# Normalised rows and the first two decoding steps, computed by ScalarE in place of VectorE

## What is computed

```python
x = _layernorm(x + attn(x))          # 16 heads of 8 channels, causal, q and k rms-normed and rotated
x = _layernorm(x + ffn(x))
# ffn: xn = rmsnorm(x) * norm_w; q = xn @ w_q.T
#      per head: top 8 of 32 scores on each of two sides, top 8 of their 64 sums -> fs, expert number fi
#      hidden = gelu(xn . expert_down[fi]) * relu(fs);  out = sum of hidden * expert_up[fi]
# _layernorm(x) = (x - mean) / sqrt(var + 1e-5)
```

## Time and profile before

| | us |
|---|---|
| three runs | 1857.17, 1856.44, 1856.55 (median 1856.55) |
| the profiled execution | 1853.35 |
| its span, first to last instruction | 1851.6 |
| granted TensorE clock, mean | 0.819 |

### The profile page before, as it was taken

One profiled execution on the slowest core, in us unless ns is written; L12 is line 12 of the kernel. 1 busy time (PEld: TensorE's weight loads), 2 busy tenths in 40 slices (PEclk: granted clock), 3 DMA queues, 4 the chain that ended last, 5 costly groups with the idle time before them and its releaser, 6 DMA issues. The chain is left out here.

```text
span 1851.6 us, 53652 instructions
## 1 busy us (share of the span) xinstructions
PE 1331.8 (72%) x19632; PEld 922.5 (50%) x19632; DVE 1554.3 (84%) x7082; ACT 891.2 (48%) x1518; POOL 732.0 (40%) x1088
## 2 busy tenths in 40 slices
PE   3557687685877768597776959678685867868646
PEld 2333364563555455455544636455463645546436
DVE  2148999888998888889888898988889898898995
ACT  1656645445554544555454455545455554554110
POOL 1125363433445343344434344442444434353230
PEclk9778789796978969697896969879697987979665
DMA  2000000000000000000000000000000000000000
GB/s 74 1 7 8 7 10 7 15 7 15 8 1 16 7 15 7 15 8 1 16 7 15 8 7 10 7 16 7 15 8 2 15 7 16 1 14 2 8 1 14
DMA packets 30049, 19.61 MB, mean 11 GB/s; under 512 B 1824, under 2 KB 29216, under 8 KB 29728
## 3 DMA queue, kind: packets, MB, share of 16 engines
q1 hardware_dynamic: 29728, 15.23, 3.0%
HBM read 11.04 MB, written 4.19 MB: 8 GB/s over the span
## 5 line engine op out<-in xcount | busy, mean ns | idle before, releaser
L579 ACT ACTIVATE prob<-S 128x512 f32<-128x512 f32 x640 | 368.7, 599 | 436.2 <-PE S L749 270.1
L841 PE MATMUL G<-whot,onehot 128*128 128x16 bf16 x12288 | 379.3, 172 | 59.2 <-DVE hid L1233 24.3
L841 PEld LDWEIGHTS G<-whot,onehot 128*128 128x128 bf16 x12288 | 365.2, 100 | 91.9 <-issue 37.4
L1195 DVE TENSOR_TENSOR onehot<-lo_no,esel 128x1024 bf16<-128x1024 uint16 x512 | 387.2, 811 | 0.1
L747 PE MATMUL S<-qT,kT_even 128*128 128x512 bf16 (+3 forms) x512 | 153.0, 329 | 146.0 <-issue 100.3
L416 POOL TENSOR_TENSOR qk_a<-qk_n,cosw 128x256 f32<-128x256 f32 x64 | 58.1, 908 | 470.4 <-DVE qk_n L1012 433.9
L462 POOL TENSOR_TENSOR gat<-gat,cande 128x1280 f16<-128x1280 f16 x64 | 151.5, 2367 | 212.1 <-DVE gat L1156 212.1
L699 PE MATMUL S<-ident_b,stack 128*128 128x128 bf16 x1024 | 100.0, 270 | 146.6 <-POOL stack L432 113.4
L749 PE MATMUL S<-causal,ident_b 128*128 128x128 bf16 x1024 | 205.4, 233 | 0.0
L699 PEld LDWEIGHTS S<-ident_b,stack 128*128 128x128 bf16 x1024 | 84.1, 124 | 185.8 <-POOL stack L432 138.2
L1136 DVE FIND_INDEX8 topi<-topv,sims 128x8 uint16<-128x32 f32 x1024 | 166.2, 187 | 0.3 <-issue 0.3
(11 more groups left out here) (139 smaller groups left out, 2578.3 us busy)
## 6 DMA issues: line engine op xcount, KB each, us to landing
xa<-in_L_attn_x SPq DMA_DIRECT2D x16, 256.0 KB, 2.7
xr<-in_L_attn_x SPq DMA_DIRECT2D x16, 256.0 KB, 3.4
out<-r SPq DMA_DIRECT2D x16, 256.0 KB, 2.4
onehot<-in_L_ffn_expert_down SPq DMA_DIRECT2D x1, 512.0 KB, 6.0
up<-in_L_ffn_expert_up SPq DMA_DIRECT2D x1, 512.0 KB, 7.1
onehot<-in_L_ffn_keys SPq DMA_DIRECT2D x1, 256.0 KB, 6.4
onehot<-in_L_attn_w_qkv SPq DMA_DIRECT2D x1, 192.0 KB, 4.8
onehot<-in_L_attn_w_proj SPq DMA_DIRECT2D x1, 64.0 KB, 4.7
```

What stands on the lines that cost most here:

```text
L579: act.activation(dst, src, ACT.Exp, scale=SCALE).then_inc(exp_done.sem, 1)
L841: last = nc.tensor.matmul(bank[:, 16 * i:16 * i + 16], onehot[:, pair, t, :], whot[:, t, w_part, :], start=(w_part == 0), stop=(w_part == 2))
L1195: dve.tensor_tensor(onehot[:, pair, t:t + 8, :].rearrange("p t (c i) -> p t c i", i=2), lo, e, ALU.is_equal)
```

## The change

Three pieces of work go from VectorE to ScalarE:

1. The kept rows of the first norm and the output rows of the second: in place of (row - mean) * root on VectorE, ScalarE computes root * row + shift with `Identity`, its scale and its bias both columns of 128x1. The shift is -mean * root, one new VectorE instruction of 128x4 for each norm: in `norm1` behind the rows `yi`, and behind `normalise(nxt, 1)` for the second. ScalarE's eight instructions stand behind the first four exponentials of group 0, first `oldest`, then `late`.
2. The first two steps of `decode`: ScalarE's `selection(late)`, a copy to integers and a Relu, stands behind the 40th exponential of b and ahead of `attended(b, 3)`. VectorE's first step of `decode` is now the mask L1180, behind a wait for ScalarE.
3. ScalarE's loop begins at b = 3 in place of 2, since its iteration now names `oldest` too. The last batch's output rows are ScalarE's too.

```diff
+            def selection(b):
+                act.wait_ge(f_ready.sem, f_filled(b, "sel"))
+                act.wait_ge(hot_done.sem, hot_done.value(b, 0))
+                bank = bank_f("sel")
+                n = 2 * P
+                act.activation(eint.rearrange("p a t c -> p (a t) c"),
+                               bank[:, 0:n].unsqueeze(2).to_broadcast([P, n, 2]), ACT.Copy)
+                act.activation(wpart[:, 0].rearrange("p a t c -> p (a t) c"),
+                               bank[:, n:2 * n].unsqueeze(2).to_broadcast([P, n, 2]), ACT.Relu).then_inc(dec.sem, 1)
...
+            def norm1_rows(b):
+                act.wait_ge(shift1_done.sem, shift1_done.value(b, 1))
+                act.wait_ge(kept.sem, kept.value(b, 0))
+                for t in range(NT):
+                    last = act.activation(y_new[:, t, :], r1[:, t, :], ACT.Identity, scale=rs[:, 0, t:t + 1],
+                                          bias=shift1[:, t:t + 1])
+                last.then_inc(ln1.sem, 1)
+
+            def norm2_rows(b):
+                act.wait_ge(shift2_done.sem, shift2_done.value(b, 1))
+                for t in range(NT):
+                    last = act.activation(r2[:, t, :], r2[:, t, :], ACT.Identity, scale=qk_rs[:, 64 + t:65 + t],
+                                          bias=shift2[:, t:t + 1])
+                last.then_inc(out_ready.sem, 1)
...
                 for g in range(NG):
                     if b is not None:
                         exps(b, g, range(4))
+                    if g == 0 and oldest is not None:
+                        norm2_rows(oldest)
+                    if g == 0 and late is not None:
+                        norm1_rows(late)
+                    if b is not None:
                         if g:
                             attended(b, g - 1)
                         exps(b, g, range(4, SIMS_UNIT + 2))
...
                     if b is not None:
                         exps(b, g, range(SIMS_UNIT + 2, UNITS))
+                if late is not None:
+                    selection(late)
                 if b is not None:
                     attended(b, NG - 1)
...
-            def norm1_rows(b):
-
-                dve.wait_ge(kept.sem, kept.value(b, 0))
-                for t in range(NT):
-                    last = dve.tensor_scalar(y_new[:, t, :], r1[:, t, :], mv[0][:, t, 0:1], rs[:, 0, t:t + 1],
-                                             ALU.subtract, ALU.mult)
-                last.then_inc(ln1.sem, 1)
+                dve.scalar_tensor_tensor(shift1[:, :], mv[0][:, :, 0], -1.0, rs[:, 0, :], ALU.mult, ALU.mult)\
+                    .then_inc(shift1_done.sem, 1)
...
+            def norm2_shift(b):
+                dve.scalar_tensor_tensor(shift2[:, :], mv[1][:, :, 0], -1.0, qk_rs[:, 64:64 + NT], ALU.mult, ALU.mult)\
+                    .then_inc(shift2_done.sem, 1)
...
-                dve.wait_ge(f_ready.sem, f_filled(b, "sel"))
-                dve.tensor_copy(pairs(eint[:, :, :, :]), twice(e))
-                dve.tensor_scalar(w0, twice(w), 0.0, None, ALU.max).then_inc(dec.sem, 1)
                 dve.wait_ge(dec.sem, dec.value(b, 1))
...
-                if oldest is not None:
-                    norm2_rows(oldest)
-                if late is not None:
-                    norm1_rows(late)
...
                 if nxt is not None:
                     normalise(nxt, 1, older, beside=hot(18, 20))
+                    if older is not None:
+                        norm2_shift(older)
```

More of the change, by code:

```diff
@@ L119, in attention_then_peer_layer @@
         rs_t = sb("rs_t", [P, 2, NT], fp32)
+        shift1 = sb("shift1", [P, NT], fp32)
+        shift2 = sb("shift2", [P, NT], fp32)
         y_new = sb("y_new", [P, NT, D], fp32)
@@ L226, in attention_then_peer_layer @@
         yi_done = signal("yi_done", 1)
+        shift1_done = signal("shift1_done", 1)
+        shift2_done = signal("shift2_done", 1)
         f_ready = signal("f_ready", 14)
@@ L241, in attention_then_peer_layer @@
         hi_done = signal("hi_done", 4)
-        hot_done = signal("hot_done", 4)
+        hot_done = signal("hot_done", 4, 4)
         g_ready = signal("g_ready", 8)
@@ L249, in attention_then_peer_layer @@
         out_ready = signal("out_ready", 1)
-        seeded = [out_stored, sims_done, hid_done, kept, rot_done, stack_done, exp_done, pv_done, oT_done, ln1, dec, ln2, cand_done, top1_done, g_free]
+        seeded = [out_stored, sims_done, hid_done, kept, rot_done, stack_done, exp_done, pv_done, oT_done, ln1, dec, ln2, cand_done, top1_done, g_free, hot_done]
         peak_ready = signal("peak_ready", NT * NH)
@@ L586, in attended, with iteration @@
                 act.activation(oT, OV[:, :], ACT.Copy).then_inc(oT_done.sem, 1)
-            def iteration(b, late, older, nxt):
+            def norm1_rows(b):
[11 more added lines that the diff above has]
+                last.then_inc(out_ready.sem, 1)
+            def iteration(b, late, older, oldest, nxt):
                 for g in range(NG):
@@ L641, in iteration @@
                     transposed(nxt, 3)
[L643 to L650, removed]
+            iteration(None, None, None, None, 0)
+            iteration(0, None, None, None, 1)
+            iteration(1, 0, None, None, 2)
+            iteration(2, 1, 0, None, 3)
+            with act.Fori(3, BATCH - 1) as b:
+                iteration(b, b - 1, b - 2, b - 3, b + 1)
+            iteration(BATCH - 1, BATCH - 2, BATCH - 3, BATCH - 4, None)
+            iteration(None, BATCH - 1, BATCH - 2, BATCH - 3, None)
+            iteration(None, None, BATCH - 1, BATCH - 2, None)
+            norm2_rows(BATCH - 1)
         @block.tensor
@@ L1115, in norm2_root @@
                              b - (BATCH - 3), 0)
[L1117 to L1122, removed]
             def top_keys(b, t):
@@ L1172, in decode @@
                 flat = lambda a: a.rearrange("p a t c -> p (a t c)")
-                e, w = bank[:, 0:n], bank[:, n:2 * n]
+                w = bank[:, n:2 * n]
                 w0, w1, w2 = (pairs(wpart[:, i]) for i in range(3))
                 rest = wrest[:, :, :].rearrange("p a t -> p (a t)")
-                dve.wait_ge(f_ready.sem, f_filled(b, "sel"))
-                dve.tensor_copy(pairs(eint[:, :, :, :]), twice(e))
-                dve.tensor_scalar(w0, twice(w), 0.0, None, ALU.max).then_inc(dec.sem, 1)
                 dve.wait_ge(dec.sem, dec.value(b, 1))
@@ L1328, in _ @@
             iteration(None, None, BATCH - 1, BATCH - 2, None)
-            norm2_rows(BATCH - 1)
 _INS = ["L0_attn_x", "L0_attn_w_qkv", "L0_attn_w_proj", "L0_attn_q_norm_w", "L0_attn_k_norm_w", "L0_ffn_w_q",
```

## The result

The changed kernel takes 1900.02 us (median of four runs, 1893.27 to 1906.24), the kernel before 1856.49 (1856.04 to 1857.17): 43.5 us more, a ratio of 1.0233 with a 95% interval of 1.0198 to 1.0269. The forecast was 1904 in a range of 1891 to 1920. The profiled execution of the changed kernel is the slowest of the four, 1906.24 us with a span of 1904.4 and a granted TensorE clock of 0.802 (before: 0.819).

What follows compares the result with a forecast made beforehand. The prediction took a closed path through TensorE, ScalarE, VectorE and GpSimd as the bound, not VectorE's busy time. Terms 44.7 + 1.5 + 3 - 2.05 - 0.2, then +0.2, gave +47 us: 1904 us, range 1891 to 1920.

Steps and rivals of the forecast that it cites:

- The five pieces: One loop iteration's closed path: scores to decode 43.59 us, VectorE 35.22, GpSimd 13.62, TensorE's weights 8.62, its loop turn 8.13.
- The rows on VectorE: Loop start: removing eight row instructions (2.05 us) only lengthens the wait for G, gain 0; 2.05 gained once, last iteration but one.
- The rows on ScalarE: Eight instructions behind group 0's fourth exponential, 0.35 us each, mostly covered by idling before the fifth: +3 us, ends 0 and +10.
- a sign that it was wrong: Signs included the fifth exponential later by more than a microsecond, or TensorE's clock lower between last `attend` and the transposes.
- The shift: One more 128x4 VectorE instruction in `norm1`, on the path: 0.1 us fifteen times, +1.5 us.
- The two decode steps: On ScalarE behind the 40th exponential, they start VectorE's mask 2.98 us later in each of 15 iterations: +44.7 us.
- A: Rival: VectorE is the bound, so work removed from it makes the kernel faster, about 1813 us; chance 0.05.
- B: Rival: no change, the selection's 3.0 us are absorbed by slack, about 1857 us; chance 0.04.
- C: Rival: TensorE idles 3 us more before the projections and falls to 1.2 GHz more often: +22, 1926 us; chance 0.05.
- D: Rival: Relu and Identity need extra ScalarE table loads at the rows and the selection: +58, 1962 us; chance 0.02.
- E: Rival: some iterations have another path, so only half of the selection's 3.0 us counts: +23, 1880 us; chance 0.04.
- The wait's length: VectorE's wait on ScalarE ahead of the mask L1180 was to appear in 15 iterations at 5 to 6 us.

Runs made afterwards that it cites:

- sel_only: The kernel before with only the two decode steps moved to ScalarE, behind the 40th exponential, rows still on VectorE: 1898.36 us, ratio 1.0233.
- extra_path: `rows_only` plus three useless 128x512 reductions on VectorE behind one-hot 11, in the 15 iterations with attention: 1880.54 us, 26.9 above `rows_only`.
- reorder_rows: `rows_only` with four one-hots taken out of VectorE's piece between decode and L1012, the second pair's 16 behind quarters 0 and 1: 1819.73 us, ratio 0.9811.
- rows_only: The changed kernel with both decode steps back on VectorE, rows and shifts still on ScalarE: 1853.66 us, ratio 0.9984 to the kernel before.
- reorder_only: The kernel before, rows on VectorE, with the one-hot order of `reorder_rows`: 1824.68 us, ratio 0.9836 to the kernel before.
- the pair of extras: `rows_only` with three useless VectorE reductions, behind one-hot 11 (1880.54 us) or at the start of VectorE's iteration (1856.29 us).

## Why the prediction was right, point by point

**What bounds the kernel.** The five pieces and their lack of slack held. A delay or a saving of 2 to 3 us in the first piece (`sel_only`) or in the second (`extra_path`, `reorder_rows`) showed in the iteration's sum with its size, and the other pieces stayed within 0.4 us.

**The rows on VectorE, 0 in the loop.** Right: the iteration of `rows_only` is not shorter, and its wait for G is longer. The gain outside the loop was mis-sized: 2.05 in the sum, 6.3 us in the traces of before and `rows_only`. The step that failed is the count of places without cover. I counted the last iteration but one; in the iterations of b = 2 and b = 15 VectorE did not wait for G either in the kernel before, and there the mask comes 2.2 and 1.2 us sooner behind the first exponential in `rows_only` (43.6 for 45.8, 42.1 for 43.3). A part of the difference is not the rows' at all: before, L855 took 9.28 us in the iteration without a next batch and VectorE waited 1.17 for it, a wait that the trace of `rows_only` lacks.

**The rows on ScalarE, +3 us.** The size of one was right, and the wait that was to cover them was misread. ScalarE's timeline at the loop's start in the changed kernel:

```profile
810.00 0.60 ACT L595 ACTIVATE prob<-S 128x512 f32<-128x512 f32 x1 [0.58 <-PE S L789]
810.49 1.64 ACT L615 ACTIVATE r<-r,shift,qk_rs 128x128 f32<-128x128 f32 x4
812.03 1.64 ACT L608 ACTIVATE y_new<-xr,shift,rs 128x128 f32<-128x128 f32 x4
813.56 0.58 ACT L595 ACTIVATE prob<-S 128x512 f32<-128x512 f32 x1
814.34 0.60 ACT L595 ACTIVATE prob<-S 128x512 f32<-128x512 f32 x1 [0.20 <-PE S L789]
```

Eight instructions take 3.07 us, 0.384 each; the prediction had 0.35. The Trainium skill, page "ScalarE: Activation LUTs", section "What ACT_TABLE_LOAD costs", gives 186 ns plus 0.833 ns per element, 93 ns more for each column operand and an overlap of 93 ns; the estimate by that is 479 ns of duration and 386 between starts, and the trace agrees: 0.48 and 0.384.

The prediction took both rows for the fifth exponential. They are the sixth. In the iteration at 780 the fifth is at 786.19, and ScalarE idled 0.68 us ahead of it, not 2.47; TensorE then makes two similarity products before the sixth score (ScalarE's and TensorE's timelines of the kernel before):

```profile
786.19 0.60 ACT L579 ACTIVATE prob<-S 128x512 f32<-128x512 f32 x1 [0.68 <-PE S L749]
```

```profile
786.63 2.06 PE L795 MATMUL F<-simW,xn 128*128 128x512 f32 x2
```

So the rows do delay the fifth exponential. Counted from the first one it starts 5.72 us behind in the kernel before and 8.13 in the changed kernel and in `rows_only` (means of the loop's twelve iterations). That is 2.4 us later, where the prediction had named more than a microsecond as a sign that it was wrong. The delay is absorbed one step on, in the long wait ahead of the sixth (2.47 before, 0.20 in the lines above): the sixth is 0.5 us later (8.80 in `rows_only`, 8.31 before), the 40th 0.2 (45.59 and 45.42). The other pair with the same order of work, `reorder_only` and `reorder_rows`, has 0.2 at the 40th too (45.19 and 45.37). Fifteen times 0.2 is the 3 us of the sum, but it rests on a misread row, and the clock's scatter (below) is larger than 0.2, so the agreement is in part luck.

With the gains outside the loop, the rows as a whole are worth 3.6 us by the medians of `rows_only`, where the sum had a loss of about 2.4 (3 + 1.5 - 2.05). That difference is small beside the interval of the changed kernel, but the sign was wrong.

**The shift, +1.5 us.** From 877.63 to 877.71, 0.08 us, fifteen times 1.2. The piece that it stands in nevertheless became 0.19 us shorter: before, VectorE idled 0.28 us once in a root step behind its own result, and that idling is gone. It is gone in `sel_only` too, which has no shift and takes 33.64 us for the piece; against that the changed kernel's 33.70 leaves 0.06 for the shift. Why the idling went was not tried.

**The two decode steps, +44.7 us.** Right in mechanism and size: 2.99 us in the iteration shown, 3.00 in the mean of `sel_only`, 41.1 us on the clock. The operations themselves took 0.59 and 0.60 us, as the copy from which they were taken.

**The rivals.** A (VectorE's sum) is excluded by `rows_only`, by the pair of extras and by the reordered kernels. B fell with the result. C came true in its premise and not in its price. TensorE idles 3.69 us ahead of the transposes of group 3's output, in place of 0.71, and in most iterations the first projections behind this pause run slower. The iteration of b = 3, in the kernel before and in the changed one:

```profile
397.13 0.63 PE L772 MATMUL A<-ident,yi 128*128 128x128 f32 x4 [0.71 <-DVE r L1054]
397.60 1.46 PE L690 MATMUL S<-wqkvT,xT 128*128 128x384 f32 x4
```

```profile
408.04 1.09 PE L812 MATMUL A<-ident,yi 128*128 128x128 f32 x4 [3.69 <-DVE r L1094]
408.92 2.77 PE L730 MATMUL S<-wqkvT,xT 128*128 128x384 f32 x4
```

The windows at these places, first before, then changed (length, busy times of the engines, clock):

```profile
397.00:399.00 2.00, 1.86 (x8) 1.07 (x8) 2.00 (x4) 0.55 (x3) 0.00 (x0) 1.00 0.45 131
408.00:410.00 2.00, 1.96 (x6) 1.59 (x7) 2.00 (x4) 0.00 (x0) 0.00 (x0) 0.50 0.00 0
```

The granted clock is 1.00 there before, 2.4 GHz, and 0.50 in the changed kernel, 1.2 GHz. The first four projections took 1.46 us in all twelve loop iterations before, and 1.98 to 2.77 in nine of twelve in the changed kernel. In the 28 us behind the last exponential the lower level was granted for 3.1 us before and for 5.9 in the changed kernel (means of twelve). This too was among the prediction's signs of being wrong, and it happened without harm: VectorE's piece, which runs beside it, did not grow (33.70, before 33.89), nor did the way to the transposes (13.69, before 13.62). The prediction had let C's cost decide by how much of it the other waits cover, and here they cover all of it.

D did not happen: ScalarE loads 30 tables in either kernel. For E the first piece grew in all loop iterations.

**The wait's length.** I had expected 5 to 6 us ahead of the mask; it is 6.35. VectorE's removed steps (1.32 us) count as waiting too, next to the old 1.71 and the 3.24 by which the mask is later behind the first exponential: 6.27 together.

## What to carry to other kernels

Before work is taken off the busiest engine, ask at which wait the saved time will arrive: here 1.8 us of added work at a loop's start came out of a wait for another engine and cost 2.6 us over the kernel, and the same work behind the mask cost 27. When a wait is to cover something, count the instructions up to it: here it stood one exponential further on than was read. Work given to an idle engine inherits the place in that engine's queue; behind five more exponentials it cost 46 us, ahead of them nothing. When the path is known, moving off it what nobody awaits yet (here half of the one-hots) brings more than moving work between engines.

## What the runs showed of the hardware that was not expected

**The moment at which TensorE's clock rises scatters, and with it the time.** At an iteration's start a 128-column product takes 0.31 us, later 0.22. Counted from the first exponential, the change comes after 7.2 to 10.8 us in the kernel before (twelve batches, mean 9.1), and the distance from first exponential to mask follows it, 43.3 to 44.6 us (correlation 0.8). Two stretches of 10 us from the start of a loop iteration in the kernel before, one with an early rise and one with a late one:

```profile
455.40:465.40 10.00, 9.09 (x170) 6.95 (x171) 7.69 (x38) 4.46 (x8) 0.00 (x0) 0.62 0.21 58
889.20:899.20 10.00, 8.54 (x132) 5.96 (x133) 6.91 (x37) 3.21 (x6) 0.00 (x0) 0.50 0.21 57
```

The first has a clock of 0.62, a mixture of 1.2 and 2.4 GHz, the second 0.50, all at 1.2 GHz. In the profiled execution of the changed kernel the rise is late in eleven of twelve batches (mean 10.4), which fits that this execution is the slowest of its four and that its first piece is 0.48 us longer than that of `sel_only` (mean 9.2). That this scatter makes the spread of 13 us between its runs is an inference: it was not seen in more than one execution of a kernel.

**The turn of a loop costs TensorE some 8 us and VectorE 2.5 to 3.9 us** in which nothing that the profile shows is waited for (TensorE 7.7 to 8.6 in the twelve turns of the kernel before, together with the branch on `far_scores` ahead of each). In the last iteration of the loop, which leaves it, TensorE's was 3.2 us. It is a piece of the path in every kernel here, 96 us in all before, and none of these runs changed it.
